# Moving a residual join between two attention stages into their neighbouring slots, and splitting a prologue's buffer clearing

## The reference, cut to what matters

```python
x = L0_attn_x                                             # 4 batches x 256 tokens x 256, f32
x = x + layernorm(attention_1(layernorm(x)))              # 16 heads of 16, causal
x = x + layernorm(ffn(layernorm(x)))

def ffn(h0):
    h = rmsnorm(h0, ln1_w)
    q, k, v = h @ Wq, h @ Wk, h @ Wv                      # 32 query heads, 4 key heads of 128
    o = causal_attention(rope(q), rope(k), v) @ Wo        # attention 2
    x = h0 + o
    t = rmsnorm(x, ln2_w)
    return x + moe(t) + shared(t)                         # 32 experts, 8 chosen, plus a shared one
```

## Time and profile before

| | |
|---|---|
| median of 3 runs | 960.92 us (959.73 to 962.18) |
| the profiled execution | 961.15 us |
| its span | 959.1 us |
| mean granted TensorE clock | 0.969 |
| busy: PE, DVE, ACT, POOL | 870.1, 624.5, 569.9, 456.0 us |
| prologue | 0 to 25.3 us |
| attention 1 | 25.4 to 182.7 us |
| attention 2's block, up to its first scores | 183.0 to 213.4 us |

### The profile page before, as it was taken

One profiled execution on the slowest core, in us unless ns is written; L12 is line 12 of the kernel. 1 busy time (PEld: TensorE's weight loads), 2 busy tenths in 40 slices (PEclk: granted clock), 3 DMA queues, 4 the chain that ended last, 5 costly groups with the idle time before them and its releaser, 6 DMA issues. The chain is left out here.

```text
span 959.1 us, 18782 instructions
## 1 busy us (share of the span) xinstructions
PE 870.1 (91%) x6108; PEld 804.9 (84%) x6108; DVE 624.5 (65%) x1620; ACT 569.9 (59%) x1572; POOL 456.0 (48%) x480
## 2 busy tenths in 40 slices
PE   4699999467999999999999999978999999999994
PEld 2589899456999998999899999967888888888884
DVE  7366666656788788877778777765545444444546
ACT  4788888455776766667666676654443334333333
POOL 5633334156766776777766777720222222221221
PEclk9999999778999999999999999997999999999998
DMA  6000100311114111141111111200433333333321
GB/s 210 23 1 24 44 23 1 99 34 38 41 46 134 44 44 35 44 134 45 33 46 40 40 46 45 51 1 17 142 116 110 99 114 103 110 115 115 104 88 44
DMA packets 50246, 63.34 MB, mean 66 GB/s; under 512 B 5728, under 2 KB 36064, under 8 KB 50176
## 3 DMA queue, kind: packets, MB, share of 16 engines
q1 hardware_dynamic: 49088, 61.41, 21.9%
q10 hardware_dynamic: 1088, 1.05, 0.3%
HBM read 41.86 MB, written 1.18 MB: 45 GB/s over the span
## 5 line engine op out<-in xcount | busy, mean ns | idle before, releaser
L637 POOL TENSOR_TENSOR b_prob<-b_prob,b_rsum 128x256 f32<-128x256 f32 (+1 forms) x128 | 104.9, 840 | 111.0 <-DVE b_rsum L619 111.0
L73 PE MATMUL banks<-act_t,b_w 128*128 128x256 f32 (+1 forms) x392 | 130.1, 332 | 1.9 <-DVE moe_hid L1994 1.0
L75 PE MATMUL banks<-act_t,b_w 128*128 128x256 f32 (+1 forms) x392 | 128.0, 327 | 0.0
L74 PE MATMUL banks<-act_t,b_w 128*128 128x256 f32 (+1 forms) x392 | 127.9, 326 | 0.0
L1898 ACT ACTIVATE moe_hid<-banks 128x512 fp32r<-128x512 f32 x66 | 39.5, 598 | 124.2 <-DVE banks L1989 124.2
L1298 ACT ACTIVATE b_prob<-banks,b_negmax 128x128 f32<-128x128 f32 (+1 forms) x256 | 103.6, 417 | 14.1 <-DVE b_negmax L1285 14.0
L1982 DVE TENSOR_TENSOR moe_gated<-banks,moe_share 128x512 f32<-128x512 f32 x66 | 45.6, 691 | 85.4 <-PE banks L75 81.8
L1156 ACT ACTIVATE b_qt<-b_work 128x512 fp32r<-128x512 f32 x64 | 40.4, 632 | 90.0 <-POOL b_work L1151 90.0
L1151 POOL TENSOR_TENSOR b_work<-b_work 128x512 f32<-128x512 f32 x64 | 86.6, 1353 | 9.5 <-DVE b_work L1139 0.4
L637 POOL TENSOR_TENSOR a_prob<-a_prob,a_rsum 128x256 f32<-128x256 f32 x64 | 51.6, 828 | 81.4 <-DVE a_rsum L619 81.4
L1147 POOL TENSOR_TENSOR b_work<-b_work,rope_t 128x512 f32<-128x512 f32 x64 | 83.2, 1300 | 7.9 <-DMA b_work<-b_work 7.9
(11 more groups left out here) (229 smaller groups left out, 3041.4 us busy)
## 6 DMA issues: line engine op xcount, KB each, us to landing
b_work<-b_work SPq DMA_DIRECT2D x128, 128.0 KB, 2.3
moe_share<-gates SPq DMA_DIRECT2D x32, 512.0 KB, 3.6
b_w_raw<-in_b_wq SPq DMA_DIRECT2D x4, 1024.0 KB, 5.4
b_w_raw<-in_b_wo SPq DMA_DIRECT2D x4, 1024.0 KB, 9.1
a_src_t<-act_t SPq DMA_DIRECT2D x5, 512.0 KB, 2.9
moe_w_raw<-in_wg SPq DMA_DIRECT2D x16, 128.0 KB, 2.2
moe_w_raw<-in_wu SPq DMA_DIRECT2D x16, 128.0 KB, 2.3
moe_w_raw<-in_wd SPq DMA_DIRECT2D x16, 128.0 KB, 2.2
```

What stands on the lines that cost most here:

```text
L73: nc.tensor.matmul(out, w_lo, m_hi, start=start, stop=False, skip_group_check=skip)
L74: nc.tensor.matmul(out, w_hi, m_lo, start=False, stop=False, skip_group_check=skip)
L75: return nc.tensor.matmul(out, w_hi, m_hi, start=False, stop=stop, skip_group_check=skip)
L637: last = self.m.nc.gpsimd.tensor_tensor(rows, rows, rsum[:, :, t:t + 1].to_broadcast([PART, 2, width]), ALU.mult)
```

## The change

The clearing: the prologue clears only the first half of `q_stack` (2,048 columns) and `k_stack` (1,024). POOL clears `v` (4,096 columns) and the second half of `q_stack` (2,048) at the start of attention 1, ahead of `acc`; `kt` is no longer cleared. ACT waits for these before the first write of `v` and before the first unit of iteration 1.

The join: callbacks after each slot of iterations 6 and 7 (k = -8 to -1) and of the drain (k = 0 to 4) carry the join of batches 0 and 1, with POOL instead of ACT applying attention's norm. Its rows lie in the first half of `q_stack` during attention 1. The join of batches 2 and 3 stands in attention 2's opening and its slots 0, 1 and 2; the transposes of batches 2 and 3 use banks 6 and 7. PE's wait for all batches before the slots is replaced by waits at first use.

```diff
-            nc.gpsimd.memset(m.b_w[:, 2 * B_W:4 * B_W].bitcast(F32), 0.0)
-            nc.gpsimd.memset(m.q_stack[:].bitcast(F32), 0.0)
+            nc.gpsimd.memset(m.q_stack[:, 0:NTT * HPI * PART].bitcast(F32), 0.0)
+            k_at = 2 * B_W + 2 * NTT * HPI * PART
+            nc.gpsimd.memset(m.b_w[:, k_at:k_at + NTT * HPI * STACK].bitcast(F32), 0.0)
...
     def act_values(self, act, it):
+        if isinstance(it, int) and it == 0:
+            wait(act, self.zeroed, 1)
...
     def act_unit(self, act, it, u):
+            if isinstance(it, int) and it == 1:
+                wait(act, self.zeroed, 2)
...
         @block.gpsimd
+            nc.gpsimd.memset(self.v.rearrange("p a t h n -> p (a t h n)").bitcast(F32), 0.0).then_inc(self.zeroed, 1)
+            nc.gpsimd.memset(m.q_stack[:, NTT * HPI * PART:].bitcast(F32), 0.0).then_inc(self.zeroed, 1)
             nc.gpsimd.memset(m.acc[:], 0.0).then_inc(self.y_added, 1)
...
+            def after(k):
+                if k == -5:
+                    pool.wait_ge(self.qt_full, PAIRS * (self.ITS - 1))
+                    join.pool_attention(pool, 0)
+                if k == -4:
+                    join.pool_attention(pool, 1)
+                if k in (2, 3):
+                    join.gpsimd(pool, k - 2)
...
         @block.tensor
+            def after(k):
+                if k in (3, 4):
+                    if k == 3:
+                        pe.wait_ge(self.exp_done, 2 * PAIRS * self.ITS)
+                    join.turn.tensor(pe, k - 3)
...
         @block.scalar
-            for b in range(NB - 1):
-                m.norm_a.roots(act, b)
+            def after(k):
+                if k == -6:
+                    m.norm_a.roots(act, 0)
+                    m.norm_a.roots(act, 1)
+                if k == 0:
+                    join.norm_f.roots(act, 0)
+                    join.norm_f.roots(act, 1)
+                    m.norm_a.roots(act, 2)
+                if k in (1, 2):
+                    join.act_input(act, k - 1)
+                if k in (3, 4):
+                    join.turn.scalar(act, k - 3)
...
         @block.vector
+            def after(k):
+                if k in (-8, -7, -2):
+                    b = {-8: 0, -7: 1, -2: 2}[k]
+                    m.norm_a.moments(dve, b, lambda t: acc[:, t, :], arrived)
+                if k == -6:
+                    m.norm_a.factors(dve, 0)
+                    m.norm_a.factors(dve, 1)
+                if k in (-4, -3):
+                    join.dve_add(dve, k + 4)
+                if k == 1:
+                    join.norm_f.factors(dve, 0)
+                    join.norm_f.factors(dve, 1)
+                    m.norm_a.factors(dve, 2)
+                if k == 4:
+                    join.turn.vector(dve, 0)
+            self.run(dve, self.slot_dve, middles, after)
+            join.turn.vector(dve, 1)
...
  class AttentionB(Attention):
         @block.gpsimd
-            self.join.gpsimd(pool, 0)
-            self.join.gpsimd(pool, 1)
             self.pool_kv(pool, 0, self.KV0)
             self.pool_kv(pool, 0, self.KV1)
-            self.join.gpsimd(pool, 2)
             self.pool_rotate(pool, 0)
-            self.join.gpsimd(pool, 3)
             self.pool_rotate(pool, 1)
-            self.slots(pool, self.slot_pool, {})
+            join = lambda b: self.join.gpsimd(pool, b)
+            self.slots(pool, self.slot_pool, {("first", 0): ((join, 2),), ("first", 1): ((join, 3),)})
...
         @block.tensor
-            turn.tensor(pe, 0)
-            pe.wait_ge(turn.lo_done, 1)
             self.pe_kv(pe, 0, self.KV0)
-            turn.tensor(pe, 1)
             self.pe_kv(pe, 0, self.KV1)
             self.pe_queries(pe, 0)
-            turn.tensor(pe, 2)
             self.pe_queries(pe, 1)
-            turn.tensor(pe, 3)
             self.pe_kv(pe, 0, self.KT)
             self.pe_queries(pe, 2)
-            pe.wait_ge(turn.lo_done, NB)
...
             self.slots(pe, self.slot_pe, {
+                ("first", 1): ((turn_h, 2),), ("first", 2): ((turn_h, 3),),
...
         @block.scalar
-            pipeline(self.join.scalar(act), work)
+            join.act_attention(act, 2)
+            self.act_kv(act, 0, self.KV0)
+            m.norm_a.roots(act, 3)
+            self.act_kv(act, 0, self.KV1)
+            join.norm_f.roots(act, 2)
+            self.act_raw(act, 0)
+            join.act_attention(act, 3)
+            self.act_raw(act, 1)
+            join.act_input(act, 2)
+            self.act_kv(act, 0, self.KT)
+            join.norm_f.roots(act, 3)
+            m.load_table(act, ACT.Exp)
+            self.act_queries(act, 0)
             self.act_raw(act, 2)
-            self.act_queries(act, 0)
...
             self.slots(act, self.slot_act, {
+                ("first", 0): ((input_h, 3),), ("first", 1): ((turn_h, 2),), ("first", 2): ((turn_h, 3),),
...
         @block.vector
-            pipeline(self.join.vector(dve), work)
+            m.norm_a.moments(dve, 3, lambda t: join.acc[:, t, :])
+            join.dve_add(dve, 2)
+            self.dve_kv(dve, 0, self.KV0)
+            m.norm_a.factors(dve, 3)
+            self.dve_kv(dve, 0, self.KV1)
+            join.norm_f.factors(dve, 2)
+            self.dve_cos(dve, 0)
+            join.dve_add(dve, 3)
+            self.dve_cos(dve, 1)
+            self.dve_kv(dve, 0, self.KT)
+            join.norm_f.factors(dve, 3)
             self.dve_queries(dve, 0)
             self.dve_cos(dve, 2)
...
             self.slots(dve, self.slot_dve, {
+                ("first", 1): ((turn_h, 2),), ("first", 2): ((turn_h, 3),),
...
+    def pool_attention(self, pool, b):
+        pool.wait_ge(self.norm_a.ready, b + 1)
+        for t in self.tiles(b):
+            last = self.m.nc.gpsimd.tensor_scalar(self.rows[:, t, :], self.acc[:, t, :],
+                                                  self.norm_a.factor[:, 0, t:t + 1],
+                                                  self.norm_a.shift[:, 0, t:t + 1], ALU.mult, ALU.add)
+        last.then_inc(self.attn_ready, 1)
+    def dve_add(self, dve, b):
+        x, rows = self.m.x, slice(NTT * b, NTT * (b + 1))
+        dve.wait_ge(self.attn_ready, b + 1)
+        self.m.nc.vector.tensor_tensor(x[:, rows, :], x[:, rows, :], self.rows[:, rows, :],
+                                       ALU.add).then_inc(self.x1_ready, 1)
+        self.norm_f.moments(dve, b, lambda t: x[:, t, :], lambda t: dve.wait_ge(self.x1_ready, b + 1))
```

More of the change, by code:

```diff
@@ L1002, in arrived @@
                 dve.wait_ge(self.y_added, 2 * (t // NTT + 1) + 1)
-            def moments(k):
-                if k < NB - 1:
-                    m.norm_a.moments(dve, k, lambda t: acc[:, t, :], arrived)
-            self.run(dve, self.slot_dve, middles, moments)
-            for b in range(NB - 1):
-                m.norm_a.factors(dve, b)
+            def after(k):
[15 more added lines that the diff above has]
+            join.turn.vector(dve, 1)
 W_DMAS = 4
@@ L1182, in pe_kv @@
         wait(pe, self.w_ready, 4 * (it // NB) + 3)
+        if it < NB:
+            wait(pe, self.join.turn.lo_done, it + 1)
         if u == self.KV0:
@@ L1309, in pe_values @@
         wait(pe, self.o_ready, P)
+        if P == 0:
+            wait(pe, self.join.turn.lo_done, 3)
         pt = lambda part: self.prob_t[:, p % 2, part, :]
@@ L1320, in pe_project @@
         wait(pe, self.o_ready, P + 1)
+        if P == 0:
+            wait(pe, self.join.turn.lo_done, NB)
         if p == 0:
@@ L1474, in slots @@
             slot(eng, P)
-            for stage, b in plan.get(P - self.STAGES, ()):
+            for stage, b in plan.get(P - self.STAGES, ()) + plan.get(("first", P), ()):
                 stage(b)
@@ L1657, in scalar, with use_rows @@
[L1657 to L1673 removed]
+    def use_rows(self, rows):
+        self.rows = self.turn.src = rows.rearrange("p (t d) -> p t d", t=NT)
@@ new lines, in act_attention @@
+    def act_attention(self, act, b):
+        for t in self.tiles(b):
+            last = self.norm_a.apply(act, self.rows[:, t, :], self.acc[:, t, :], t)
+        last.then_inc(self.attn_ready, 1)
+    def dve_add(self, dve, b):
[4 more added lines that the diff above has]
+        self.norm_f.moments(dve, b, lambda t: x[:, t, :], lambda t: dve.wait_ge(self.x1_ready, b + 1))
@@ L1675, in gpsimd, with act_input @@
+    def act_input(self, act, b):
+        for t in self.tiles(b):
+            last = self.norm_f.apply(act, self.rows[:, t, :], self.m.x[:, t, :], t, 1)
+        last.then_inc(self.turn.rows_ready, 1)
     def gpsimd(self, pool, b):
```

84 lines of the change are left out of this document (26 added, 58 removed).

## The result

The changed kernel takes 947.37 us (median of 4 runs, 944.96 to 950.87) against 961.27 for the kernel before in the same session; the ratio is 0.986, with a 95% interval of 0.9826 to 0.9894: faster, by 13.9 us. 950.0 was predicted.

What follows compares the result with a forecast made beforehand. PE, busy 91% of the span, was taken as the bound, with gains where it stands still: prologue and join. Terms -7.3 + 0.5 + 7.7 + 1.6 - 15.8 + 2.2 = -11.1 took 961.15 to 950.0 us, chance 0.55 for 946 to 954.

Steps and rivals of the forecast that it cites:

- (a): Prologue: less clearing frees DVE's 128x2 operation, restart at about 18.1 instead of 25.37 us; -7.3 us, bounds -8.5 and -5.
- (b): Attention 1's opening: POOL's moved clearing delays the first normalisation about 3.1 us, mostly covered; +0.5 us, bounds 0 and +3.1.
- The rival in which the clearing returns: Attention 1's opening: clearing costs its bound of +3.1, or DVE's copy waits 2.2 for the memset; near 952.5 us, chance 0.08.
- (c): Attention 1's last slots: added moments, table loads and DVE additions lengthen them; +7.7 us, bounds +3 and +12.
- waiting for POOL: Slot k = -4: DVE's two-operand SBUF addition waits up to 1.6 us for POOL's work, within that slot's +2.9.
- (d): Drain after attention 1: table load moves into ACT's idle time, factors and two PE turns are added; +1.6 us, bounds 0 and +3.
- (e): Attention 2's opening: first scores 14.5 us after block start instead of 30.3; -15.8 us, bounds -17.5 and -12.
- (f): Attention 2's first slots: added turns, input and POOL pieces, POOL's second piece +0.8 and DVE's lock; +2.2 us, bounds 0 and +5.
- The tail was covered: Rival: DVE's and ACT's extra work in attention 1's last slots overlaps better, +3 instead of +7.7; 945.3 us, chance 0.15.
- POOL did not take the gain back: Rival judged: POOL's chain sets attention 2's first slots, opening and slots together give -7 instead of -13.6; 956.6 us, chance 0.12.
- No drain behind a table load: Rival judged: ACT stands still 1.28 us after each of two added table loads in attention 1; 952.6 us, chance 0.05.
- The slower rival: PE's clock falls to half in attention 1's stretched slots from k = -6 on, +15 us; 965 to 970 us, chance 0.05.

Runs made afterwards that it cites:

- clear_only: The kernel before with only the change's lighter prologue clearing, its join left as before; 956.4 us, ratio 0.9943 to the kernel before.
- load_ahead: Changed kernel with the next weights' load issued in attention 1 instead of at the start of attention 2; 945.42 us, ratio 0.9827 to the kernel before.
- join_only: Changed kernel with all clearing back in the prologue, as before; 954.62 us, ratio 0.9925 to the kernel before.
- pieces_later: Changed kernel with POOL's two join pieces after slots 4 and 5 of attention 2 instead of 0 and 1; 950.64 us, ratio 0.9861.
- load_ahead_pieces: load_ahead with both of POOL's join pieces behind slot 0 of attention 2; 944.04 us, ratio 0.9808 to the kernel before.
- changed_again: The changed kernel, unaltered, timed again beside the variants; 948.33 us, ratio 0.9847 to the kernel before.
- swaps_three_first: Changed kernel with the next weights' load issued behind the swaps of pairs 0, 1 and 2; 946.36 us, ratio 0.9832 to the kernel before.
- swaps_first: Changed kernel with the next weights' load issued behind the first two query tiles' swaps; 946.55 us, ratio 0.9842 to the kernel before.

## Why the prediction came out right, and where its terms were off

**(a)** The mechanism was right: the operation at 5.4 us in 0.17, the restart by 20. The size was 1.1 us short. The step "the chain behind it moves up 8.6 us and would end near 16.7" failed, since tiles of `x` hold the moments until 7.55 us, and the chain ends at 18.96; I had that as a bound. The load landed 1 us later than the 17.8 of before. That the load is a limit of its own was shown by the profile of `clear_only`, where the restart is 1.6 us behind DVE's end.

**(b)** +1.0 against +0.5. The cover held: the normalisation is 2.9 us later (3.1 predicted), and PE waits 0.20 for it. The terms given leave 5.3 - 1.5 = 3.8 us of delay and not 3.1, so that number was better than its working. The same stretch grew by 1.1 in `clear_only` and by 0.8 in `load_ahead`, and not in `join_only` (111.5), which points to the clearing; but `pieces_later` and `load_ahead_pieces`, with the lighter clearing, have 111.5 and 111.6 too, so it is not a fixed price of it. All of the growth lies before the eleventh slot (50.5 us from the restart before, 51.5 in the changed kernel, 50.4 in those two). In the changed kernel it is the slots of pairs 1 to 4, 1.1 us longer in sum, with clocks of 0.50 to 0.87 where before only the first of them was under 1.00; in `clear_only`, `changed_again` and `load_ahead` it is the time to the first scores, 8.2 us instead of 7.4. What makes an execution take one or the other is open. The rival in which the clearing returns was wrong, and the copy's 0.28 us shows why.

**(c)** +5.3 against +7.7 (its four terms add up to 7.8), inside its bounds. With the slots at the full clock of `swaps_three_first` it comes apart: moments behind a unit +0.8 (predicted +1.1), table loads +2.3 (+2.4), DVE's additions and moments +0.9 and +0.7 (+2.9 and +1.4), and PE's half clock +0.8, which had no place in the sum. The step that failed is the waiting for POOL "up to 1.6 us". DVE's additions took 0.73 and 0.66 us here, about the 0.69 of the earlier trace rows, and it was POOL that took longer beside the first of them, 1.54 us for its piece instead of 1.10. Of DVE's small operations before the maxima, the one behind the first addition took its 0.17 us, that behind the second 0.46, and that of batch 2's moments 0.83.

**(d)** +1.0 against +1.6, the table load and the turns as described.

**(e)** -14.1 against -15.8. The forecast's own terms add up to 9.9 + 2.7 + 0.6 + 0.7 = 13.9 us and not to its 14.5; from POOL's start to the scores it was 4.5 and not 4.0. The step that was mis-sized is the landing: swap issued at 188.16, earlier than taken because PE ran at the full clock at the block's start, and landed 7.2 us later, where the longest row of before was 5.1. I took 9.9 us in the block for it, POOL could start at 11.7. `load_ahead` and the two variants built on it confirm that the load is the cause, with 2.4 for the longest landing in each.

**(f)** +2.0 against +2.2, and the agreement is in good part luck. 1.3 us are the slot of pair 0 at the lower clock, which no term of (f) had. Whether the longer stop before it (6.46 against 2.47) brings that or the execution's chance is open, since `clear_only` shows it without the new join, behind 2.94: its pair 4 comes 26.5 us after the first scores, only 0.5 sooner than in the changed kernel. With that slot set aside, what is left of (f) is +0.7 (20.6 us for slots 1 to 3 against 19.9 before and 20.0 in `clear_only`): the slot with the stop for POOL's keys grew by 0.7, as the stop went from 4.67 to 5.62, and the two before it cancel. So the second piece of POOL was priced about right at +0.8, and the rest of the +2.2, DVE's lock, adds nothing: one rotation of POOL's took 2.38 us instead of 1.3 there, but before one had taken 2.19. `pieces_later` and `load_ahead_pieces` showed that POOL's pieces are what lengthens the stop (4.67 and 4.66 without them in front of it).

**The sum.** By the profiled execution the sum was -10.3 against -11.1; by the medians it was -13.9, 2.6 us more than the forecast, and `changed_again`'s profile has -12.7. The terms missed on both sides, (c) by 2.4 us one way, (a) and (e) by 1.1 and 1.7 the other, and this cancelling is luck too. Attention 1's block took 165.0 us, between the 162 of a covered tail and the 167 forecast.

**The rivals.** The tail was covered in part. POOL did not take the gain back: 27.0 us, where more than 31 would have shown it. In the three other places of the load the slots took back a third of what the join won, but there it is the late swap that POOL waits for (6.16 us in `swaps_first`). No drain behind a table load: both roots stand at the load's end, 146.80 behind 145.51 + 1.28. The Trainium skill (ScalarE: Activation LUTs, section What ACT_TABLE_LOAD costs) adds a drain of 1.38 us to each load, which would have the root at 148.2; the measurement decides. The slower rival's mechanism, PE's clock falling in the stretched slots, did happen, from the place that I had named, but there for one slot and 0.8 us net (and 1.3 us more in attention 2's slot of pair 0), not six slots and 15: the windows show it back at 0.83 in the second half of that slot and at 1.00 in the next.

## What to carry to other kernels

The time of a small transfer on the critical path (here 128 KB, 2.3 us) depended on what stood beside it in the DMA engines, not on its queue: put a large prefetch where no one waits for a small copy, in an earlier stage if its buffer is free there. Room read off a plain slot does not hold for a slot with more work in it; read the chain of that very slot. Moving POOL's pieces among the slots behind the join shortened one stop by 0.95 us and lengthened slot 7 by 0.9 to 1.2. Before a change in a slot's time is put down to an edit, look at PE's granted clock in it: a slot in which PE is busy from end to end took 3.6 to 6.6 us here with the same matmuls, and two profiles of unchanged instructions there (`clear_only` and the kernel before) lay 1.4 us apart.

## What had not been expected of the hardware

A swap's DMA of 128 KB that took 2.3 us alone took 6.8 to 7.3 beside a load of 2.3 MB, on the same queue and on another. The granted clock fell to 0.50 behind stops of 1.24 and 1.59 us in eight of nine profiles and stayed at 1.00 in one, with the same instructions, which makes up to 2 us of difference between executions there. DVE's small operations on 128x4, each waiting for the one before, follow at 0.20 us, of which 0.16 are the operation.
